# A graph and mixture-of-experts layer on one core: the last eight weight chunks are quantized and turned inside the first expert tiles

## The reference

```python
x = x + gnn(layernorm(x), adj, adj)   # adj_n = dinv (sym(adj) + I) dinv;  y = adj @ (adj_n @ xn)
x = x + ffn(layernorm(x), ...)        # below, per token

def _bit_quant(W):                    # per row of W
    scale = clip(mean(abs(W), axis=-1), 1e-05)
    return clip(round(W / scale), -1, 1) * scale
h = layernorm(x) * gamma + beta
shared_out = silu(h @ sw1.T) @ sw2.T                 # sw1: 1024 x 512, sw2: 512 x 1024
probs = softmax(h @ router_w.T)                      # 8 experts, the best one per token
eo = silu(h @ ew1[e].T) @ ew2[e].T
out = shared_out + top_prob * eo[top_idx]
```

## Time and profile before

| | us |
|---|---|
| median of 3 runs | 705.63 |
| the three runs | 699.36, 705.63, 707.7 |
| profiled execution | 702.86 |
| its span | 701.2 |
| TensorE busy | 648.4 (92%) |
| VectorE busy | 469.2 (67%) |
| ScalarE busy | 389.6 (56%) |
| GpSimd busy | 151.7 (22%) |
| granted TensorE clock, mean | 0.991 of full speed |

### The profile page before, as it was taken

The page is one execution under the profiler, slowest core; times in us unless marked ns, Lnnn a source line. Parts: engine busy times, 40 slices in busy tenths (PEclk is TensorE's granted clock), DMA queues, the critical chain, the costliest instruction groups (busy, mean ns, idle before and its releaser), DMA issues.

```text
span 701.2 us, 15954 instructions
## 1 busy us (share of the span) xinstructions
PE 648.4 (92%) x5281; PEld 381.6 (54%) x5281; DVE 469.2 (67%) x1031; ACT 389.6 (56%) x726; POOL 151.7 (22%) x171
## 2 busy tenths in 40 slices
PE   0798999999979999999998789999999999999995
PEld 0343444444434554445434367777767677777773
DVE  4878988566664555688788669756855565555553
ACT  1658648879986776777657653333432242424241
POOL 2234430000000000012323206200021353434322
PEclk9999999999999999999999999999999999999999
DMA  8999962675897777866576896643284876868641
GB/s 348 417 421 417 421 255 62 194 196 155 237 242 251 264 259 253 282 225 237 175 270 218 241 248 166 173 111 96 76 141 131 197 195 176 187 185 181 177 141 31
DMA packets 107103, 151.68 MB, mean 216 GB/s; under 512 B 64286, under 2 KB 64286, under 8 KB 102944
## 3 DMA queue, kind: packets, MB, share of 16 engines
q1 hardware_dynamic: 91280, 117.74, 53.5%
q0 software_dynamic: 6960, 20.99, 9.9%
q10 hardware_dynamic: 8800, 12.09, 5.7%
HBM read 119.57 MB, written 19.16 MB: 198 GB/s over the span
## 4 chain that ended last, share of the span: by engine, by line
PE 54%; DMA 14%; DVE 13%; ACT 9%; issue 7%; SPq 1%; POOL 1%; DVEq 0%; ACTq 0%; POOLq 0%
PE bank L1545 16%; PE bank L1517 16%; PE bank L1390 7%; PE bank L1392 7%; PE bank L1391 7%; DMA region<-in_adj_t 6%; ACT junk L748 4%; DMA work<-in_w 3%; ACT region L760 2%; DVE work L1096 2%; DVE region L986 2%; PE bank L1421 2%; DMA work<-in_adj_t 1%; DVE region L1192 1%; DVE region L982 1%
## 5 line engine op out<-in xcount | busy, mean ns | idle before, releaser
L1545 PE MATMUL bank<-region,work 128*128 (+1 forms) x624 | 141.6, 379 | 4.4 <-DVE work L1244 4.2
L886 ACT ACTIVATE work<-work 128x512 f32<-128x512 f32 x78 | 48.5, 622 | 171.1 <-DVE work L1234 171.1
L1390 PE MATMUL bank<-zreg,work 128*128 (+1 forms) x256 | 98.2, 384 | 12.3 <-DVE work L1164 10.9
L1517 PE MATMUL bank<-zreg,region 128*128 128x128 f16 x1728 | 100.9, 219 | 0.0
L1517 PEld LDWEIGHTS bank<-zreg,region 128*128 (+1 forms) x1728 | 98.1, 98 | 4.2
L1391 PE MATMUL bank<-zreg,work 128*128 (+1 forms) x256 | 98.2, 384 | 0.0
L1392 PE MATMUL bank<-zreg,work 128*128 (+1 forms) x256 | 98.0, 383 | 0.0
L1390 PE MATMUL bank<-region,work 128*128 128x512 f16 x192 | 74.1, 386 | 25.4 <-DVE region L1010 25.4
L1545 PEld LDWEIGHTS bank<-region,work 128*128 128x128 f16 x624 | 58.9, 98 | 70.4 <-issue 7.4
L748 ACT ACTIVATE junk<-work 128x512 f16<-128x512 f32 x124 | 77.6, 625 | 15.9 <-DMA work<-in_w 13.8
L1244 DVE SCALAR_TENSOR_TENSOR work<-work 128x512 f16<-128x512 f32 x78 | 53.7, 691 | 48.8 <-ACT work L893 48.8
(11 more groups left out here) (154 smaller groups left out, 946.8 us busy)
## 6 DMA issues: line engine op xcount, KB each, us to landing
work<-in_w SPq DMA_DIRECT2D x62, 512.0 KB, 4.1
region<-in_adj SPq DMA_DIRECT2D x16, 1024.0 KB, 10.7
region<-in_adj_t SPq DMA_DIRECT2D x16, 1024.0 KB, 7.5
work<-in_adj_t SPq DMA_DIRECT2D x32, 384.0 KB, 4.4
zreg<-s_scratch SPq DMA_DIRECT2D x24, 256.0 KB, 3.9
xb<-in_w SPq DMA_DIRECT2D x10, 512.0 KB, 4.2
zreg<-in_x SPq DMA_DIRECT2D x4, 1024.0 KB, 9.7
h_scratch<-hb POOLq DMA_DIRECT2D x16, 256.0 KB, 3.4
```

Source lines behind the costliest of these rows:

```text
L886: nc.scalar.activation(h1[:, cols], pre[:, cols], ACT.Silu).then_inc(h1_ok, 1)
L1390: nc.tensor.matmul(dst, a_hi, b_hi, start=start, stop=False, skip_group_check=True)
L1517: last = nc.tensor.matmul(ps_h[b][f // 4][:, (f % 4) * P:(f % 4 + 1) * P], w, ht[n % RING][:, c:c + P], start=(f % 4 == 0 and d == 0 and h ...
L1545: last = nc.tensor.matmul(ps_y[b][:, :].rearrange("p (d c) -> p d c", d=DB), h1hl[:, b, h, f * P:(f + 1) * P], w, start=(f == 0 and h == 0 ...
```

## The change

Chunks 64 to 71 no longer belong to macros 10 and 11 of the second product. They go through the shared tiles: SP loads them into two areas that are free by then (`late_raw`: a part of `zreg`, and the second half of `raw` once x1's tiles 14 and 15 are normalized). ScalarE takes the sums of chunk i in tile i + 2, VectorE writes the integers in tile i + 3 into the area of gamma and beta (`late_words`), SP turns them with a transposing transfer issued in the same tile, and ScalarE writes the signs in tile i + 6. On ScalarE sums and signs stand after the tile's own operations and the next base load, in front of the wait for `y_ok`; on VectorE a ternary stands between the halves of a tile, after the routing there. The loads of x's rows 12 to 15 move in front of the two transposing loads of h, two macros earlier in SP's order. The last part of the scales goes out after tile 12. GpSimd's third iota waits for the last ternary. The loops over tiles on VectorE and ScalarE are written out for tiles 2 to 11. TensorE waits for all signs before the first routed tile.

```diff
+        late_raw = [zf[:, 4 * D:6 * D], raw[:, 1, :]]
...
+        late_words = gb[:, :, :].rearrange("p a d -> p (a d)").bitcast(I16).rearrange("p (b n) -> p b n", b=2)
...
+        LATE_MACROS = 2
+        LATE_FROM = 2 * CHUNKS - LATE_MACROS * STEPS
+        LATE_TILE = 3
...
         def by_dma(q):
-            return isinstance(q, int) and q < EARLY_CHUNKS and q % 2 == 1
+            return isinstance(q, int) and (q >= LATE_FROM or q < EARLY_CHUNKS and q % 2 == 1)
...
+        def weight_free(m):
+
+            return isinstance(m, int) and (m == IDLE or m >= MACROS - LATE_MACROS)
...
             for m in range(IDLE, MACROS - 1):
                 macro(2, m, False)
+            for b in range(2):
+                sp.wait_ge(tern_ok, LATE_FROM - 1 + b)
+                sp.dma_start(raw[:, b, :].rearrange("p (t d) -> p t d", d=D), x_t[:, 12 + 2 * b:14 + 2 * b, :]
+                             ).then_inc(xz_in[b], 16)
             for n in range(2):
                 load_shared(n)
             macro(2, MACROS - 1, False)
-            for b in range(2):
-                sp.wait_ge(tern_ok, 2 * CHUNKS - 1 + b)
-                sp.dma_start(raw[:, b, :].rearrange("p (t d) -> p t d", d=D), x_t[:, 12 + 2 * b:14 + 2 * b, :]
-                             ).then_inc(xz_in[b], 16)
...
+            def load_late(i):
+
+                q, kind, c = late(i)
+                if i == 0:
+                    sp.wait_ge(p2_step, 3 * NT)
+                elif i == 1:
+                    sp.wait_ge(ln_normed, NT)
+                else:
+                    sp.wait_ge(tern_ok, q - 1)
+                if kind == 1:
+                    sp.dma_start(late_raw[i % 2].rearrange("p (a d) -> p a d", a=2),
+                                 w1_c[c, :, :, :]).then_inc(late_loaded[i % 2], 16)
+                else:
+                    sp.dma_start(late_raw[i % 2], w2_c[c, :, :]).then_inc(late_loaded[i % 2], 16)
+
+            def turn_late(i):
+
+                q, kind, c = late(i)
+                dst = (w1t if kind == 1 else w2t)[:, ds(c * CHUNK, CHUNK)]
+                sp.wait_ge(tern_ok, q + 1)
+                sp.dma_start(dst.bitcast(I16).rearrange("p (k r) -> p k r", r=P), late_words[:, i % 2, :], transpose=True
+                             ).then_inc(late_turned[i % 2], 16)
+
+            load_late(0)
             for n in range(RING, NT):
                 load_shared(n)
+                turning = n - RING - LATE_TILE
+                if turning >= 0:
+                    turn_late(turning)
+                if -1 <= turning < LATE_MACROS * STEPS - 2:
+                    load_late(turning + 2)
+            turn_late(7)
...
-            act.wait_ge(abs_ok, 4 * CHUNKS)
+            act.wait_ge(abs_ok, 2 * LATE_FROM)
...
+            def late_weights(n):
+
+                if 0 <= n - LATE_TILE + 1 < LATE_MACROS * STEPS:
+                    i = n - LATE_TILE + 1
+                    act.wait_ge(late_loaded[i % 2], 16 * (i // 2) + 16)
+                    sums(late(i), i % 2, late_raw[i % 2])
+                if 0 <= n - LATE_TILE - 3 < LATE_MACROS * STEPS:
+                    i = n - LATE_TILE - 3
+                    store_w(late(i), i % 2)
+
             def shared_tile(n, r):
 
                 tile(n, r % 2, min(n, 2) if isinstance(n, int) else 2)
                 if not (isinstance(n, int) and n < 2):
                     next_base(n, r % 2)
+                late_weights(n)
                 if not (isinstance(n, int) and n == 0):
                     shared_store(n - 1, (r + 1) % 2)
...
-            store_s2(2, 4, EARLY0, S2_FROM[2])
-            with act.Fori(1, ROUTE_TILE // 2) as i:
-                for b in range(2):
-                    shared_tile(2 * i + b, b)
+
+            for n in range(2, ROUTE_TILE):
+                shared_tile(n, n % 2)
...
                 if n == ROUTE_TILE:
                     store_gate()
+                    store_s2(2, 4, EARLY0, S2_FROM[2])
...
-            turn_s2(2, 2 * CHUNKS)
             norm_parts(1, 12)
...
+            def late_ternary(i):
+
+                ternary(late(i), i % 2, late_raw[i % 2], i < 2)
+
+            for n in range(3, AHEAD + 1):
+                shared_tile(n, n % 2, [2 * n], [(route, 2 * n - 1), (late_ternary, n - LATE_TILE)])
+            for n in range(AHEAD + 1, ROUTE_TILE - 1):
+                shared_tile(n, n % 2, [n + AHEAD], [(late_ternary, n - LATE_TILE)])
+            turn_s2(2, 2 * CHUNKS)
...
-            pe.wait_ge(wt_ok, 2 * CHUNKS)
+            pe.wait_ge(wt_ok, LATE_FROM)
             logits(0)
...
+            pe.wait_ge(wt_ok, 2 * CHUNKS)
             pe.wait_ge(unit_ok, 1)
```

More of the change, by code:

```diff
@@ L304, in build @@
         s2t_ok = sem("s2t_ok")
+        late_loaded = [sem("late_loaded0"), sem("late_loaded1")]
+        late_turned = [sem("late_turned0"), sem("late_turned1")]
         pool_waits = sem("pool_waits")
@@ L348, in by_dma, with turned_by, late @@
         def by_dma(q):
-            return isinstance(q, int) and q < EARLY_CHUNKS and q % 2 == 1
+            return isinstance(q, int) and (q >= LATE_FROM or q < EARLY_CHUNKS and q % 2 == 1)
+        def turned_by(q):
+            if q < EARLY_CHUNKS:
+                return turned, 16 * (q // 2) + 16
+            return late_turned[q % 2], 16 * ((q - LATE_FROM) // 2) + 16
+        def weight_free(m):
+            return isinstance(m, int) and (m == IDLE or m >= MACROS - LATE_MACROS)
+        def late(i):
+            return later(2, (LATE_FROM - EARLY_CHUNKS + i) // STEPS, i % STEPS)
         def turn_count(q):
@@ L450, in macro @@
                         turn(EARLY_CHUNKS - 3 + 2 * s)
-                    if not (isinstance(m, int) and m == IDLE):
+                    if not weight_free(m):
                         load_w(later(g, m - (g == 2), s), s % 2)
@@ L819, in macro @@
                         store_w(early(ROUNDS - 1, s - LAG + early_count(ROUNDS - 1)), (s - LAG) % 2)
-                    elif not (first or isinstance(m, int) and m == IDLE + 1):
+                    elif not (first or isinstance(m, int) and weight_free(m - 1)):
                         store_w(later(g, mm - 1, s - LAG + STEPS), (s - LAG) % 2)
-                    if not (isinstance(m, int) and m == IDLE):
+                    if not weight_free(m):
                         act.wait_ge(raw_loaded[b], 32 * mm + 16 * (s // 2) + 16)
@@ L871, in _ @@
                 macro(2, m, False, 2 * m - 12)
-            for s in range(STEPS - LAG, STEPS):
-                store_w(later(2, MACROS - 2, s), s % 2)
-            act.wait_ge(abs_ok, 4 * CHUNKS)
+            act.wait_ge(abs_ok, 2 * LATE_FROM)
             nc.scalar.activation(junk[:, 0:1], power[:, 0:1], ACT.Silu)
@@ L1085, in ternary @@
                     if by_dma(q - 2):
-                        dve.wait_ge(turned, 16 * ((q - 2) // 2) + 16)
+                        dve.wait_ge(*turned_by(q - 2))
                     else:
@@ L1469, in macro @@
                     idle = isinstance(m, int) and m == IDLE
-                    if s and not (late_turn or idle):
+                    if s and not (late_turn or weight_free(m)):
                         turn_w(later(g, m - (g == 2), s - 1), (s - 1) % 2, False)
@@ L1473, in macro @@
                         turn_w(early(ROUNDS - 1, early_count(ROUNDS - 1) - 1), 1, False)
-                    elif s == 0 and not (isinstance(m, int) and m == IDLE + 1):
+                    elif s == 0 and not (isinstance(m, int) and weight_free(m - 1)):
                         turn_w(later(g, m - 1 - (g == 2 and not idle), STEPS - 1), 1, False)
@@ L1499, in _ @@
                 macro(2, m, m == IDLE)
-            turn_w(later(2, MACROS - 2, STEPS - 1), 1, False)
             def columns_in(n):
```

18 lines of the change are left out of this document (6 added, 12 removed).

## The result

| | before | changed |
|---|---|---|
| median, us (20 runs each) | 702.54 | 694.74 |
| lowest to highest | 699.24 to 707.7 | 692.07 to 702.27 |
| profiled execution | 702.86 | 702.27 |
| its span | 701.2 | 700.6 |
| ratio of the runs, 95% interval | | 0.9892, 0.987 to 0.9915 |

The change gains 1.1%, 7.8 us between the medians. The forecast was 693.3, in a range of 686 to 702. But the profiled execution of the changed kernel is the slowest of its 20 runs and stands 7.5 us above their median. So its trace shows the gain and, further on, what can eat it.

A forecast was written before the change was run, and what follows sets the result against it. TensorE was taken as the bound wherever fed, with waits in the second product's last two macros. 702.86 less 10.6 (9.3 there, 1.3 in the tail) gave 692.3, said as 693.3 for the four-execution mean; range 686 to 702.

The forecast's parts named there:

- The second product: Its last two macros were to take 23.0 in place of 32.3 us, starting the first product 9.3 us earlier.
- Step 9's wait: In the second product's last two macros, TensorE's 1.32 us wait behind a pair of ScalarE sums was to go.
- Step 11: In the second product's last two macros, a 1.5 us wait for the low part was to stay.
- step 12: In the second product's last macro, the 2.79 us wait for a queued load was to shrink to 0.8 us.
- the last macros keep their waits: Rival for the second product: norm chain and SP's queue keep the waits, only 5.5 us gained, 698; chance 0.15.
- VectorE in tiles 3 to 10: One added 1.44 us ternary per shared tile was to cost 0, with ends of 0 and 4.3 us.
- The rival in which VectorE becomes the bound: In tiles 3 to 10 VectorE's added work gives 4.3 us back, 697.6; chance 0.12.
- Table loads: Rival: ScalarE loads tables around each Sign in the shared tiles, 5 us lost in tiles 6 to 9, 698; chance 0.03.
- Tiles 3 to 10 at no cost: Work and transfers added to the shared tiles were to hide under TensorE on VectorE, ScalarE and SP, costing 0.
- The term put at 0: The cost of the late work and its transfers in the shared tiles, taken as 0 us in the sum.
- The slower rival: In tiles 4 to 9 ScalarE stands at `late_loaded` for late loads, 19.8 us lost, 712; chance 0.05.
- The place in front of `y_ok`: In shared tiles ScalarE's sums and signs run while VectorE makes that output, so the base store isn't later: 0.

The follow-up runs named there:

- again: The changed kernel unaltered, timed and profiled a second time (the second comparison) against the kernel before: 692.73 us, ratio 0.9855.
- nodma: Changed kernel without the eight late turning transfers and six of the eight late weight loads, engine work kept: 691.34 us, ratio 0.9825 to the kernel before.
- order: Changed kernel with ScalarE's late sums and signs behind the wait for `y_ok` and the base store: 699.93 us, ratio 0.9968 to the kernel before.
- sp_base: Changed kernel with SP instead of ScalarE issuing the base loads of tiles 2 to 9: 694.9 us, ratio 0.9848 to the kernel before.
- best: Changed kernel with the alterations of swap and sp_base together, nothing else: 689.37 us in 5 runs, ratio 0.982 to the kernel before.
- after: The first profiled execution of the changed kernel, unaltered, slowest of its 20 runs: 702.27 us.
- swap: Changed kernel with SP issuing a routed tile's scale load ahead of the gathered-rows load three tiles on: 690.85 us, ratio 0.9823 to the kernel before.
- one_macro_b: Changed kernel moving only chunks 68 to 71, x loads back behind the last macro's loads: 699.65 us, ratio 0.9964 to the kernel before.
- none: Changed kernel without late loads, sums, ternaries or turning transfers, only the eight signs kept: 695.24 us, ratio 0.9849 to the kernel before.
- noturn: Changed kernel without the eight late turning transfers and the waits for them: 694.35 us, ratio 0.9855 to the kernel before.
- noload: Changed kernel without six of the eight late weight loads (chunks 66 to 71 reuse data): 692.58 us, ratio 0.9851 to the kernel before.
- plain_copy: Changed kernel with the late turning transfers replaced by untransposed copies of the same bytes: 694.3 us, ratio 0.9834 to the kernel before.
- one_macro: Changed kernel moving only chunks 68 to 71, x loads kept in their early place: 707.82 us, ratio 1.0035 to the kernel before.

## Why the prediction was right, and where it was not

**The second product: right.** The two macros were to take 23.0 us in place of 32.3; they took 22.6 in both traces (376.66 to 399.24, in again 377.88 to 400.44). Step 9's wait went. Step 11 kept 1.06 us in both traces (forecast 1.5), step 12 kept 0.36 and 0.34 (forecast 0.8). On SP's queue the x loads took 0.95 us and the two transposing loads behind them 4.69, done at 382.3 (forecast 383.1). From the first product to second_product(0) it is 8.67 us, forecast 8.6. second_product(0) at 407.91 and 409.1; forecast 408.7.

**The rival "the last macros keep their waits": wrong.** Its 698 lies above what came; 1.4 us of waits are left of 5.6, in both traces.

**VectorE in tiles 3 to 10: right.** In again and nodma its eight ternaries are in, and TensorE is busy 55.00 of 55.00 us. The rival in which VectorE becomes the bound is out.

**Table loads: right, none.** The eight added signs after a transfer (22 in all) last as long as the 14 before, and no load stands at one:

```profile
L808 ACT ACTIVATE region<-region 128x1024 f16<-128x1024 int16 x22 | 22.9, 1041 | 0.5 <-DMA region<-work 0.5
```

There are four table loads in the whole span, as before. By the Trainium skill ("ScalarE: Activation LUTs", section "Table sets: the hidden batching unit") Sign isn't named among the fillers; this trace shows that it runs between SiLUs without a load, so here it acts as one. Nor is the 2.7 us that the prediction quotes for a change of set reached: in order's timeline above, Exp and SiLU each start 0.01 to 0.02 us behind their load of 1.28 us.

**Tiles 3 to 10 at no cost: the step that failed.** The prediction said of the late loads and turning transfers "the traffic there is light" and asked only whether they would be late themselves. They were later than the 4.1 us put for them, 4.8 to 8.7 us in the changed kernel's trace, yet ScalarE never waits for `late_loaded` there; it comes to it late from its waits for stores. Without those, in sp_base and best, it does wait for such a load, 2.61 and 2.21 us at most, and TensorE loses nothing. What costs is that the new transfers raise the DMA share from 0.48 to 0.98, and with it the landing of transfers that were there already: base stores 2.9 to 5.2 or 7.2 us, h loads 3.3 to 4.8 or 7.8. The wait for `y_stored` in `next_base` had no place in the prediction; it cost nothing before. Nor had the landings of the base loads and of the loads of h. The term put at 0 is 0 in again and about 8 us in the profiled execution: 3.8 at tile 5, and 4.0 in the steps of 10.93 and 8.58 us at the end of the routing (8.52 and 7.02 in again). VectorE and ScalarE reach those late: the chain runs from the last store of the ladder through them to the wait at 502.82. In the median it is some 1.4 us (again less nodma), which the intervals don't establish. The slower rival had the right neighbourhood, ScalarE stopped by a transfer in these tiles, but the wrong one of its waits, and a price per load where it is a chain of stores. That a busier stretch makes landings late is shown by nodma. That this is what the slower runs lose is seen in the traces of after, swap and one_macro_b, and isn't shown for the medians.

**The place in front of `y_ok`: right.** There the late work was put at 0 because it hides, and the equal tile steps of again and none bear that out. The prediction didn't ask what the place is worth; order shows that behind the wait most of the gain would be lost, 2 to 3 us left of 10.

**Not seen: the gap at the first routed tiles.** The prediction says nothing of it. It costs 1.8 us before the change (8.64 + 7.21 less two steps of 7.03), 0.8 in again, 4.4 in the profiled execution after the change (9.68 and 8.82), 4.8 in noturn, and in the whole series of none 4 us or more, two tiles earlier and behind another wait. swap shows the order on SP's queue as the cause in its series; why the size differs so much between executions stays open, and so whether swap would close it everywhere. It also blurs the comparison of kernels 1 or 2 us apart.

**The number: near, in part by luck.** The median is 1.4 us above the forecast in the first comparison, and 0.6 below it in the second. But the forecast took its 10.6 us off a mean of 703.9 from four executions, and the kernel before has a median of 702.54 in 20 runs. As a gain, 7.8 us came in the first comparison, 2.8 less than forecast, and about 10 in the second.

## What to carry to other kernels

Work moved under a bound engine has to be checked for what its transfers do to others: list each wait for a *completion* in that stretch, on every engine, with its slack, and ask what happens if every landing doubles. A wait for a store's landing on a compute engine's instruction stream, in front of the next store, makes a chain whose period is landing plus work; let a queue issue it whose own work can stand behind that wait. On a compute engine, place filler in front of a wait it would stand in anyway, and on a DMA queue never move a load that has to wait in front of one that somebody needs.

## What the runs showed of the hardware that was not expected

- 256 KB stores to DRAM landed in 2.7 us at a DMA share of 0.48, in 3.2 and 3.5 with one kind of added traffic (noturn, noload) and in 5.2 to 7.2, at worst 10.59, at 0.96 to 0.98. The Trainium skill ("DMA: Bandwidth & Descriptors", section "Latency and other measured facts") has HBM access at 2 us under high load. That is the latency of an access, not the landing of a whole transfer: the stores here grew by more, 4.3 us in the median of the changed kernel's trace and 7.7 at worst.
- The share of busy time tells it better than the bytes: noturn, noload, plain_copy and again have 0.74, 0.77, 0.88 and 0.98 over the same 55 us, and their stores land in 3.2, 3.5, 4.3 and 5.2 us, while the rates are 188, 166, 219 and 221 GB/s. It is no law: at an equal 0.98 the landing differs by execution, 5.2 and 7.2 us, and one_macro and one_macro_b have 3.7 us at 0.85 and 4.7 at 0.81.
- Waits of 1.06 to 1.75 us left TensorE's granted clock at 1.00. After waits of 2.71 and 2.50 us it was 0.72 in the mean of the next six us (the row of 503 to 509 above), between its two levels of 1.2 and 2.4 GHz, and sixteen wide matmuls took 5.02 and 5.41 us in place of 3.62. The length of the wait alone doesn't decide: behind the 2.26 us of the kernel before they took 3.61, at a clock of 1.00, and behind 1.87 us in swap's trace 5.30. Behind the 8.14 us of one_macro it was the lower level outright:

```profile
401.00:406.00 5.00, 4.31 (x17) 2.13 (x18) 1.76 (x3) 4.45 (x7) 2.43 (x2) 0.50 0.82 133
```
